# The coarsest level of a convolution pyramid kept and multiplied as plain fp32 instead of as split fp32r parts

## The reference

```python
def basic_block(x, w1, w2, stride=1, ds=None):
    out = jax.nn.relu(conv3(x, w1, stride) * BN_S)
    out = conv3(out, w2, 1) * BN_S
    identity = conv1x1(x, ds, stride) * BN_S if ds is not None else x
    return jax.nn.relu(out + identity)
x = basic_block(x, e0b0c1, e0b0c2)
x = basic_block(x, e0b1c1, e0b1c2)
f0 = x
x = basic_block(x, e1b0c1, e1b0c2, stride=2, ds=e1b0ds)
x = basic_block(x, e1b1c1, e1b1c2)
f1 = x
x = basic_block(x, e2b0c1, e2b0c2, stride=2, ds=e2b0ds)
x = basic_block(x, e2b1c1, e2b1c2)
x = (jax.nn.relu(deconv2(x, dec0w) * BN_S) + f1) * BN_S
x = (jax.nn.relu(deconv2(x, dec1w) * BN_S) + f0) * BN_S
return x
```

## Time and profile before

| | |
|---|---|
| time of 3 runs | 90.62, 90.75, 91.16 us; median 90.75 |
| profiled execution, first to last instruction | 88.7 us |
| median less that span (launch and end) | 2.0 us |
| busy: PE, PEld, DVE, ACT, POOL | 81.9, 74.0, 63.6, 44.8, 27.4 us |
| level 2 on PE, first e2b0c1 matmul to first dec0 matmul | 71.39 to 81.29 us of the span |
| level 2, matmuls of e2 weights and identity | 31 + 3 + 12 + 12 + 2 + 12 = 72 |

### The profile page before, as it was taken

How to read it: one execution, slowest core, us unless ns; L and a number is a source line. 1 busy time by engine, 2 the same in 40 slices (tenths; PEclk the granted TensorE clock), 3 DMA queues, 4 the chain that set the end, 5 groups by cost and what they waited for, 6 DMA issues and landing times.

```text
span 88.7 us, 1554 instructions
## 1 busy us (share of the span) xinstructions
PE 81.9 (92%) x541; PEld 74.0 (83%) x541; DVE 63.6 (72%) x186; ACT 44.8 (51%) x94; POOL 27.4 (31%) x43
## 2 busy tenths in 40 slices
PE   5978999999999999999999999999999999999900
PEld 3756999998877799999978878999999999887600
DVE  5579999799968799756635478999449798542750
ACT  6007015879435065744423359799930089990410
POOL 7300070999930000753440000100885002400140
PEclk9999999999999999999999999999999999999985
DMA  2978910044782013560000000000000000000075
GB/s 23 254 209 306 342 78 0 0 119 91 194 268 76 2 23 108 159 186 5 0 0 0 0 4 0 0 0 0 0 7 0 0 4 0 7 0 0 0 267 206
DMA packets 4183, 6.51 MB, mean 73 GB/s; under 512 B 464, under 2 KB 2128, under 8 KB 4176
## 3 DMA queue, kind: packets, MB, share of 16 engines
q1 hardware_dynamic: 4032, 6.29, 23.6%
q10 hardware_dynamic: 144, 0.13, 0.4%
HBM read 5.37 MB, written 1.05 MB: 72 GB/s over the span
## 4 chain that ended last, share of the span: by engine, by line
PE 86%; DVE 4%; DMA 3%; ACT 1%; POOLq 1%; issue 1%; DVEq 0%
PE psum L830 79%; DMA x_sb<-x_in 3%; PE psum L869 3%; PE psum L967 2%; DVE stats L613 2%; POOLq L167 1%; PE psum L1022 1%; PE psum L855 1%; DVE moments L628 1%; DVE shared L642 1%; ACT result L588 0%; ACT shared L585 0%; PE psum L862 0%; DVE flat L743 0%; DVE result L616 0%
## 5 line engine op out<-in xcount | busy, mean ns | idle before, releaser
L470 POOL TENSOR_TENSOR odd<-relu,odd 128x363 fp32r<-128x363 f32 x12 | 13.6, 1149 | 15.4 <-ACT odd L545 15.3
L830 PE MATMUL psum<-shared,w_e0b0c 128*128 128x364 f32 x72 | 12.4, 331 | 0.4 <-DVE shared L642 0.4
L830 PEld LDWEIGHTS psum<-shared,w_e0b0c 128*128 128x128 f32 x72 | 11.9, 188 | 0.7 <-issue 0.7
L830 PE MATMUL psum<-shared,w_e0b1c 128*128 128x364 f32 x72 | 12.2, 329 | 0.0
L830 PEld LDWEIGHTS psum<-shared,w_e0b1c 128*128 128x128 f32 x72 | 12.1, 188 | 0.1
L830 PE MATMUL psum<-odd,w_e0b0c 128*128 128x512 f32 x48 | 11.6, 400 | 0.0
L830 PE MATMUL psum<-odd,w_e0b1c 128*128 128x512 f32 x48 | 11.6, 400 | 0.0
L758 DVE SCALAR_TENSOR_TENSOR relu<-psum,inside 128x363 f32<-128x363 f32 (+2 forms) x18 | 8.7, 489 | 3.4 <-PE psum L830 3.4
L830 PEld LDWEIGHTS psum<-odd,w_e0b1c 128*128 128x128 f32 x48 | 9.1, 189 | 2.2
L830 PEld LDWEIGHTS psum<-odd,w_e0b0c 128*128 128x128 f32 x48 | 9.1, 189 | 2.2
L545 ACT ACTIVATE odd<-relu 128x363 fp32r<-128x363 f32 x12 | 6.1, 507 | 7.1 <-DVE relu L758 7.0
(11 more groups left out here) (126 smaller groups left out, 139.6 us busy)
## 6 DMA issues: line engine op xcount, KB each, us to landing
x_sb<-x_in SPq DMA_DIRECT2D x4, 160.0 KB, 3.8
raw<-e0b0c_in SPq DMA_DIRECT2D x2, 256.0 KB, 4.8
raw<-e0b1c_in SPq DMA_DIRECT2D x2, 256.0 KB, 4.9
raw<-e1b1c_in SPq DMA_DIRECT2D x2, 256.0 KB, 2.7
raw<-e2b1c_in SPq DMA_DIRECT2D x2, 256.0 KB, 2.7
raw<-e1b0c_in SPq DMA_DIRECT2D x1, 448.0 KB, 4.1
raw<-e2b0c_in SPq DMA_DIRECT2D x1, 448.0 KB, 3.8
x_sb<-x_in SPq DMA_DIRECT2D x2, 192.0 KB, 3.8
```

The costliest lines, as they stand in the source:

```text
L470: pool.tensor_tensor(split_of(piece, 1), fp32_of(piece), split_of(piece, 0).bitcast(F32), ALU.subtract).then_inc(lo_ready, 1)
L830: last = pe.matmul(target, w, moving, start=(first and n == 0), stop=(final and n == len(terms) - 1), skip_group_check=skip)
```

## The change

1. The weights of level 2 (e2b0c1, e2b0c2, e2b0ds, e2b1c1, e2b1c2) are kept as one fp32 tile written by ACT. DVE's `weights_lo` for these five is gone, and the `raw` slots of these weights come free for the next DMA on `w_hi` instead of on `w_lo`.
2. The maps of level 2 (`planes2`, `sides2`, `corner2`, `odd2`, `flat2`) are single fp32 tiles. DVE writes each once, from the sums, and raises one semaphore, `map_ready`; the lo writes (L729, L752), the fp32 copies in `relu` (L758, second) and the subtractions (L777) of these stages are gone. e2b1c2's output alone (`last2`) is still written as hi and lo, since dec0 is multiplied as before.
3. Each product of level 2 is one `matmul` of fp32 tiles in place of three of fp32r. e2b0c1 does three of its five whole products for each image alone (`EARLY`), the other two for both images at once, then one for each side. The identity is multiplied with `eye` in fp32.
4. The side copies and corners carry one fp32 map, half the elements, and wait for `map_ready`.
5. ACT's 16 gathers of level 0's skip (L580) stand ahead of the side copies of level 2.
6. `skip1` is no longer copied by POOL: ACT writes its hi part (4 instructions, behind its corners) and POOL its lo part by subtraction (4 instructions, behind ACT's).

What PE does in levels 0 and 1, and everything from dec0 on, stays.

```diff
+EARLY = 3
+def in_parts(k):
+    return not WEIGHTS[k][0].startswith("e2")
...
+        self.whole = name == "e1b1c2" or (level == 2 and name != "e2b1c2")
...
-        split1 = sb("split1", [P, 2, IMAGES, 2, 2, MAP[2]], F32R)
+        planes2 = sb("planes2", [P, IMAGES, 2, 2, MAP[2]])
...
-        flat2 = sb("flat2", [P, 2, IMAGES, MAP[2]], F32R)
-        odd2 = sb("odd2", [P, 2, IMAGES, RUN[2]], F32R)
-        corner2 = sb("corner2", [P, 2, IMAGES, EVEN_RUN[2]], F32R)
+        flat2 = sb("flat2", [P, IMAGES, MAP[2]])
+        odd2 = sb("odd2", [P, IMAGES, RUN[2]])
+        corner2 = sb("corner2", [P, IMAGES, EVEN_RUN[2]])
+        sides2 = sb("sides2", [P, 2, IMAGES, RUN[2]])
+        last2 = sb("last2", [P, 2, IMAGES, EVEN_RUN[2]], F32R)
...
-        w_sb = [sb(f"w_{n}", [P, 2, m, P], F32R) for n, m, _ in WEIGHTS]
+        w_sb = [sb(f"w_{n}", [P, 2, m, P], F32R) if in_parts(k) else sb(f"w_{n}", [P, 1, m, P])
+                for k, (n, m, _) in enumerate(WEIGHTS)]
...
-                    wait_w_lo(sp, k - RAW_SLOTS)
+                    wait_raw_free(sp, k - RAW_SLOTS)
...
-            wait_half(pool, source_of_level(2, IMAGES - 1), 1)
-            pool.wait_ge(corner_by_dve, 1)
             for i in range(2):
+                pool.wait_ge(skip1_hi, i + 1)
                 for j in range(2):
...
-                    last = pool.tensor_copy(skip1[:, :, i, j], source.bitcast(F32))
+                    last = pool.tensor_tensor(skip1[:, 1, i, j], skip1_source(i, j), skip1[:, 0, i, j].bitcast(F32),
+                                              ALU.subtract)
                 last.then_inc(skip1_ready, 1)
...
             scale_skip0(1)
+            for image in range(IMAGES):
+                act.wait_ge(skip0_added, image + 1)
+                for q in range(4):
+                    for i in range(2):
...
+                        last = act.activation(target, source, ACT.Copy)
+                last.then_inc(skip0_ready, 1)
+
             gather_sides(2, 0)
             gather_corners(2, 0, range(2))
             gather_sides(2, 1)
             gather_corners(2, 0, range(2, 4))
             gather_corners(2, 1, range(3, 4))
-            for image in range(IMAGES):
-                act.wait_ge(skip0_added, image + 1)
...
-                last.then_inc(skip0_ready, 1)
+            for i in range(2):
+                for j in range(2):
+                    last = act.activation(skip1[:, 0, i, j], skip1_source(i, j), ACT.Copy)
+                last.then_inc(skip1_hi, 1)
...
                     for i in range(2):
-                        last = dve.tensor_scalar(planes_inside(2, 0, image, i),
+                        last = dve.tensor_scalar(planes2_inside(image, i),
...
-                    last.then_inc(hi_direct, 1)
+                    last.then_inc(map_ready, 1)
+                elif stage.name == "e2b0c2":
+                    every = sums.rearrange("p i (r c) -> p i r c", c=PITCH[2])[:, :, :, 0:BLOCKS[2]]
+                    dve.tensor_scalar(maps2_inside(), every, 0.0, None, ALU.max).then_inc(map_ready, 1)
+                elif stage.whole:
+                    dve.scalar_tensor_tensor(out=odd2[:], in0=sums, scalar=0.0, in1=mask, op0=ALU.max,
+                                             op1=ALU.mult).then_inc(map_ready, 1)
+                elif stage.name == "e2b1c2":
+                    dve.tensor_scalar(last2[:, 0], sums, 0.0, None, ALU.max).then_inc(hi_direct, 1)
                     wait_half(dve, piece.index, 0)
...
+                    dve.scalar_tensor_tensor(out=last2[:, 1], in0=sums, scalar=0.0, in1=last2[:, 0].bitcast(F32),
+                                             op0=ALU.max, op1=ALU.subtract).then_inc(lo_direct, 1)
...
-                if 0 < piece.index < len(WEIGHTS):
+                if 0 < piece.index < len(WEIGHTS) and in_parts(piece.index):
                     weights_lo(piece.index)
...
-            for piece in PIECES[:DEC0[0].index]:
+            for piece in [p for p in PIECES[:DEC0[0].index] if STAGES[p.stage].level < 2]:
...
+            def even_2(name, target, first):
+
+                k = W_INDEX[name]
+                pe.wait_ge(w_hi, k + 1)
+                wait_half(pe, LEVEL2[name].index - 1, 0)
+                products(target, [(w_sb[k][:, 0, s], shifted(odd2, s, EVEN_RUN[2])) for s in range(4)],
+                         first=first).then_inc(summed, 1)
...
+            for image in range(IMAGES):
+                wait_half(pe, source_of_level(2, image), 0)
+                for n in range(EARLY):
+                    pe.matmul(target[:, image], w[:, 0, n], whole[n][:, image], start=(image == 0 and n == 0),
+                              stop=False, skip_group_check=True)
+            products(target, [(w[:, 0, n], whole[n]) for n in range(EARLY, len(WHOLE))], first=False, final=False,
+                     skip=True)
+            pe.wait_ge(sides_by_act, 2 * IMAGES)
+            pe.wait_ge(sides_by_dve, 2 * IMAGES)
+            products(target, [(w[:, 0, len(WHOLE) + side], sides2[:, side]) for side in range(2)], first=False,
+                     skip=True).then_inc(summed, 1)
...
+            products(target, [(w_sb[W_INDEX["e2b0ds"]][:, 0, 0], corner2[:])], final=False)
+            wait_relu(pe, LEVEL2["e2b0c2"].index + 1 - BANKS)
+            warm_up(1, (LEVEL2["e2b0c2"].index + 1) % BANKS)
+            even_2("e2b0c2", target, first=False)
...
+            pe.wait_ge(skip1_ready, 1)
+            wait_w_lo(pe, W_INDEX["dec1w"])
+            skip_round(0, 0)
+            skip_round(0, 1)
...
+            products(target, [(w_sb[k][:, 0, s], shifted(flat2, s, RUN[2])) for s in range(4)]).then_inc(summed, 1)
...
+            products(target, [(eye, flat2[:, :, PITCH[2] + 1:PITCH[2] + 1 + EVEN_RUN[2]])], final=False)
+            warm_up(FILL, DEC0_BANKS[0])
+            even_2("e2b1c2", target, first=False)
```

More of the change, by code:

```diff
@@ L271, in wait_w_lo, with wait_raw_free @@
             else:
-                engine.wait_ge(w_lo, k)
+                engine.wait_ge(w_lo, sum(in_parts(j) for j in range(1, k + 1)))
+        def wait_raw_free(engine, k):
+            if in_parts(k):
+                wait_w_lo(engine, k)
+            else:
+                engine.wait_ge(w_hi, k + 1)
         def lines_of(run, level):
@@ L297, in map_inside, with plane1_inside @@
[L297 to L306, removed]
+        def plane1_inside(half, image, i, j, row=0, rows=BLOCKS[1]):
+            first = (row + 1) * PITCH[1] + 1
+            return lines_of(split0[:, half, image, i, j, first:first + rows * PITCH[1]], 1)
@@ L367, in split_of @@
                 return flat_inside(half, piece.images, piece.row, piece.rows)
-            return odd[stage.level][:, half] if stage.level == 2 else odd[1][:, half, piece.images[0]]
+            return odd[1][:, half, piece.images[0]]
         def dec0_sums(row):
@@ L756, in _ @@
+                for target, signal in [] if stage.from_bank or stage.whole else \
                         ([(split_of(piece, 0), hi_direct)] if stage.direct else []) + [(fp32_of(piece), relu_ready)]:
@@ L773, in _ @@
                     side_copies(1, 0, 2, 2)
-                if stage.direct and not stage.from_bank:
+                if stage.direct and not stage.from_bank and not stage.whole:
                     wait_relu(dve, piece.index)
@@ L832, in products @@
                 return last
-            def of_images(maps, level, first, run, images):
-                runs = maps[:, :, first:first + run]
-                return runs if level == 2 else runs[:, images[0]]
             def wait_source(piece, half):
@@ L942, in moving @@
                                       sx:sx + BLOCKS[0]]
-                    source, run = (odd, EVEN_RUN) if stage.kind == "even" else (flat, RUN)
-                    return of_images(source[level][:, half], level, sy * PITCH[level] + sx, run[level], images)
+                    source, run = (odd1, EVEN_RUN[1]) if stage.kind == "even" else (flat1, RUN[1])
+                    first = sy * PITCH[1] + sx
+                    return source[:, half, images[0], first:first + run]
                 pe.wait_ge(w_hi, k + 1)
-                if stage.name == "e2b1c1":
-                    wait_relu(pe, last_piece(STAGE["e1b1c2"], range(IMAGES), 0))
-                    pe.wait_ge(skip1_ready, 1)
-                    wait_w_lo(pe, W_INDEX["dec1w"])
-                    skip_round(0, 0)
-                    skip_round(0, 1)
-                elif stage.name == "e2b1c2":
-                    warm_up(FILL, DEC0_BANKS[0])
-                elif stage.name == "e2b0c2":
-                    wait_relu(pe, piece.index + 1 - BANKS)
-                    warm_up(1, (piece.index + 1) % BANKS)
@@ L958, in _ @@
                 if stage.kind == "down":
                     whole = [[moving(half, shifts * sy + sx) for sy, sx in WHOLE] for half in range(2)]
[L961 to L974 removed]
+                    wait_source(piece, 0)
```

188 lines of the change are left out of this document (92 added, 96 removed).

## The result

| | before | changed |
|---|---|---|
| median | 90.75 us (3 runs, 90.62 to 91.16) | 89.73 us (4 runs, 89.64 to 89.92) |
| ratio to before | | 0.9883, 95% interval 0.9863 to 0.9903 |
| span of the profiled execution | 88.7 | 87.8 (87.85 in the trace) |
| PE matmul instructions | 541 | 517 |

A fourth execution of the kernel before took 204.43 us, more than twice the others, and is in neither the median nor the ratio.

A forecast was written before the change was run, and what follows sets the result against it. PE's matmuls bound levels 0 and 1, a PE-DVE chain level 2; 0.82 + 0.29 + 0.18 + 0.29 - 0.02 = 1.56 us gained, taking the median 90.75 to 89.2 us, range 88.4 to 90.0.

The forecast's parts named there:

- The bound: PE without gap through levels 0 and 1, savings elsewhere there priced at zero; level 2 a chain of PE and DVE.
- A plain product as two records of two column times: Level 2: each fp32 product issues two matmuls, 0.134 us a record at 144 columns, 0.151 at 164.
- The two signs taken for it: From sum_stats' 72-column pair, DVE starting 0.31 us after its second record; from the hi/lo split, moving columns passing twice.
- e1b1c2's map 0.19 earlier: Ahead of e2b0c1: side copies end sooner, so DVE starts on image 1's sum at 71.60 us, before 71.79.
- e2b0c1, 0.82: Level 2's first stage: DVE starts on its sum at 74.20 us, before 75.02, gaining 0.82 us.
- The covers: Level 2's side copies, corners, skip1 and PE's fillers stay hidden; ACT over 0.9 us late before each further tenth shows.
- PE starts again 0.34 to 0.39 after DVE starts on the sum.: Between level 2's stages: this distance stays as before, since the write PE waits for keeps size and engine; change 0.
- Everything from dec0 on stays.: After level 2: dec0's first matmul to the end of the span keeps its length, predicted gain 0.
- The floor price (88.3): Level 2 records stay at 0.111 us at all widths; gain 2.47 us, time 88.3; chance 0.08.
- the dearer product (92.7): Level 2: a plain product costs more than the three it replaces, 0.22 us a record; 1.99 lost, 92.7; chance 0.06.
- The thin covers: Level 2: skip1, DVE's sides and the fillers each late by 0.1 to 0.3 us; time 89.5 to 90.0; chance 0.12.
- rival 1: Level 2 records stay on the floor, 0.111 us at all widths; gain 2.47 us, time 88.3; chance 0.08.

The follow-up runs named there:

- The order experiment: Changed kernel with ACT's 16 gathers of level 0's skip put back behind level 2's side copies, corners and skip1 writes: 89.63 us, ratio 0.9883.
- the single-wait kernel: Changed kernel with PE's wait for w_hi taken once ahead of e2b0c1, only map_ready waited for behind the fillers: 89.52 us, ratio 0.9867.
- The kernel with one wait and one memset: Changed kernel with w_hi waited for once ahead of e2b0c1, plus a one-column DVE memset in level 0 ahead of its masks: 89.16 us, ratio 0.9803.
- the ones with 2 and 19 memsets: Changed kernel with w_hi waited for once, plus 2 or 19 one-column DVE memsets in level 0: 89.17 us (0.9799) and 89.23 us (0.9807).
- the table: Changed kernel with unread plain fp32 and fp32r products of 72 to 512 columns put into level 0, giving us a record by width: 115.01 us.

## Why the prediction was right, and where it was off

**The bound.** Right: levels 0 and 1 kept their 63.4 to 63.5 us whatever was taken from or given to DVE, and level 2's chain carried the whole gain.

**A plain product as two records of two column times.** Right. The two signs taken for it (0.31 us from the last record to DVE, and the passes that the kernel's own split suggests) gave 0.134 and 0.151 us a record; measured 0.122 to 0.124 and 0.139. The term was too dear by 0.012 because it was read from fp32r rows of 290 and 364 columns, which carry 12 to 16 ns that a plain record has not. Over six steps that makes 0.06 to 0.07 us in each of the three shorter stages; the step from the first record to the second, priced at 0.17 and 0.18, took 0.20 to 0.215 and gave 0.03 back. What is left is 0.04 to 0.05 us each, 0.13 in all, in the kernel's favour.

**e1b1c2's map 0.19 earlier.** Right: DVE started on image 1's sum 0.20 after e2b0c1's first matmul, before 0.40; the side copies that had held it up ended at 70.52 + 0.62 = 71.14.

**e2b0c1, 0.82.** Measured 0.80. The long records were cheaper (six steps of 0.139 in place of 0.15, some 0.07), and two first steps were dearer: 0.175 in place of 0.11 behind the wait for image 1's map, and 0.18 in place of 0.15 into the long records.

**The covers.** All held. ACT's gathers ran from 65.23 to 70.53 and the first side copy started at 70.56, 0.07 behind the end of the write it needs (70.49); predicted were 70.45 and 70.35 on a time axis 0.17 earlier. So the gathers ended 0.04 behind that map, where the prediction had 0.1 in one place and 0.02 ahead of it in another; with the gathers last the copy follows the write by 0.03. This cover was used up, and what it cost the copies, some 0.03, PE did not see. PE's list of waits in the changed kernel names DVE's writes and nothing of ACT or POOL in level 2. The order experiment showed besides that this cover was not needed.

**"PE starts again 0.34 to 0.39 after DVE starts on the sum."** This step failed: 0.48, 0.44, 0.47. The prediction priced the write between and overlooked the wait: in the diff `w_hi` and `map_ready` stand together behind the filler, where the kernel before had one wait. It was to be read there without any trace. Cost 0.28 us gross, 0.2 net, as the single-wait kernel gives back.

**"Everything from dec0 on stays."** This failed too, by 0.36 us: the instructions stayed, their times did not. With the 21 records that DVE lost, its first result write waits 0.41 us behind a met semaphore; one instruction more on DVE, with its tile, takes the wait away, and why stays open. Nothing in the trace of before could have told the length; that the program of an engine gets shorter could be seen, and no cost in either direction was put to it.

**The rivals.** The floor price (88.3) is excluded by the spacing, the dearer product (92.7) too. The thin covers did not show. The true loss was of a kind that none of the rivals named; the range caught it since it reached to 90.0 for the covers, and that is luck. The range also was said to take in nearly all of rival 1, whose own time of 88.3 lies below its lower end of 88.4.

Mended, the sum is 1.56 + 0.13 (cheaper records) - 0.28 (waits) - 0.36 (tail) = 1.05 against 1.02 measured. The kernel with one wait and one memset has both losses undone: level 2 8.31, tail 7.42, 89.16 us, ratio 0.9803 to the kernel before. By the trace that is 1.59 us less than before, the size of gain that had been predicted for the change; the ones with 2 and 19 memsets (0.9799 and 0.9807) can't be told from it.

## What to carry to other kernels

An fp32 product as three fp32r products against one plain product is a question of width: with 128 x 128 weights, three records at the floor are 0.336 us, and a plain product is 2 x (two column times + 0.0025) once it is wider than 131 columns. By the table the plain one wins at 144 and 164 columns (0.244 and 0.278), loses at 256 (0.432 against some 0.36, an estimate with one column time and 0.013 for each fp32r record), and the two meet near 200, worked out as (0.336 / 2 - 0.0025) x 2.4 / 2 columns. So it fits the coarse levels of a pyramid and not the fine ones; besides it saves the lo writes, which are worth something only where their engine is on the chain.

On a chain of engine to engine, put behind the filler only the one wait that comes last, and take every wait that has long been met ahead of it: here that was 0.2 us for three moved lines. And when a shortened engine gives back less than the sum says, look in the chain for "issue" behind a semaphore instruction: a stall at the end may come from the length or the layout of an engine's program, and one idle instruction more is a cheap test.

## What the runs showed of the hardware that was not expected

- A plain fp32 record costs 2 to 3 ns over two column times, an fp32r record of 288 columns or more 12 to 16 ns over one. So at equal streaming (144 plain, 288 fp32r) the plain one is shorter: 0.122 against 0.132 us.
- Two semaphores waited for ahead of one matmul on PE cost 0.09 us over one, and show as a semaphore instruction of 0.05 us of its own, though one of the two had been met by 39.6 us, 35 us earlier (DVE's start to PE's product 0.476, 0.440, 0.475 against 0.383, 0.347, 0.384).
- DVE stood still for 0.41 us behind a met semaphore, ahead of its first result write, in all five traces in which its program had the changed kernel's length; in none of the five with one or more instructions (and a tile for them) added, and not in the kernel before, where 0.04 us lie between. One added instruction in level 0 was enough, and two added just ahead of the write did the same. The mechanism stays open.
